# Six more pair sums ahead of the transposes, as accumulating transfers: a convolution stage on one Trainium2 core

## The reference

```python
# layer 0: attention over channels inside 8x8 windows, then a two-layer MLP, both residual
q, k, v = to_grid(conv1x1(x, Wq, bq)), to_grid(conv1x1(x, Wk, bk)), to_grid(conv1x1(x, Wv, bv))
attn = softmax(einsum('bgck,bgcl->bgkl', q, k) / sqrt(128))
x = x + from_grid(einsum('bgkl,bgcl->bgck', attn, v))
x = x + conv1x1(gelu(conv1x1(x, W1, b1)), W2, b2)
# layer 1: a 3x3 convolution whose kernel is made anew for each pixel from 16 sets
enh  = depthwise3x3(conv1x1(x, w_pw)) + b            # padded
h    = grouped_conv3x3(x)                            # 16 channels, split in h1, h2
att  = conv1x1(h1 * h2) * attgamma + conv1x1(x, w_211)          # 16 numbers per pixel
attk = einsum('bpn,nm->bpm', att, selfw)             # 64 groups x 2 x (2*9) weights per pixel
y    = einsum('bpgij,bpgj->bpgi', attk, patches3x3(enh)) + einsum('bpn,nc->bpc', att, selfb)
x    = y * ga1 + enh + x
```

## Time and profile before

| | before |
|---|---|
| median of three runs | 5735.58 us |
| the profiled execution: its own time | 5731.75 us |
| the profiled execution: its span | 5730.0 us |
| TensorE busy, matmuls | 5581.3 us (97%) |
| VectorE busy | 5083.3 us (89%) |
| GpSimd busy | 4185.7 us (73%) |
| ScalarE busy | 3463.1 us (60%) |
| share of the DMA engines used | 22% |

### The profile page before, as it was taken

How to read it: one execution, slowest core, us unless ns; L and a number is a source line. 1 busy time by engine, 2 the same in 40 slices (tenths; PEclk the granted TensorE clock), 3 DMA queues, 4 the chain that set the end, 5 groups by cost and what they waited for, 6 DMA issues and landing times.

```text
span 5730.0 us, 115887 instructions
## 1 busy us (share of the span) xinstructions
PE 5581.3 (97%) x39944; PEld 4131.5 (72%) x39944; DVE 5083.3 (89%) x5319; ACT 3463.1 (60%) x4284; POOL 4185.7 (73%) x1831
## 2 busy tenths in 40 slices
PE   8999999999998699999999999999999999999998
PEld 7888888888886366666666766666666666766666
DVE  7888888888887789999899998989999899998989
ACT  6888888888886455455554555555455554555553
POOL 4565555555654678888888888888888888888885
PEclk9999999999999799999999999999999999999999
DMA  2222222222221222222222222222222222222221
GB/s 89 73 73 73 73 73 77 77 73 73 73 73 62 52 72 67 69 64 65 73 67 70 62 65 71 67 71 66 68 64 65 73 67 70 62 65 71 67 71 45
DMA packets 155248, 394.20 MB, mean 69 GB/s; under 512 B 35136, under 2 KB 38400, under 8 KB 155136
## 3 DMA queue, kind: packets, MB, share of 16 engines
q1 hardware_dynamic: 154800, 392.87, 22.0%
q10 hardware_dynamic: 400, 0.69, 0.1%
HBM read 219.37 MB, written 136.31 MB: 62 GB/s over the span
## 4 chain that ended last, share of the span: by engine, by line
PE 54%; DMA 8%; DVE 3%; SPq 1%; issue 1%; ACT 1%; DVEq 0%; POOLq 0%; POOL 0%; ACTq 0%
PE ps_t L888 18%; PE ps_k L871 17%; DMA xin<-layer_out 8%; PE ps_m L854 8%; PE ps_p L840 5%; PE ps_t L905 2%; DVE products L1100 2%; PE ps_t L896 1%; PE ps_t L903 1%; PE ps_m L861 1%; ACT out_sb L991 1%; SPq L736 1%; DVE products L1062 0%; SPq L684 0%; SPq L711 0%
## 5 line engine op out<-in xcount | busy, mean ns | idle before, releaser
L805 POOL TENSOR_TENSOR enh<-enh,tap 128x1280 f32<-128x1280 f32 (+1 forms) x1024 | 2512.9, 2454 | 485.2 <-ACT tap L1009 431.7
L1100 DVE TENSOR_TENSOR products<-ps_k,enh 128x1024 f32<-128x1024 f32 x1792 | 2157.4, 1221 | 269.4 <-PE ps_k L871 248.5
L871 PE MATMUL ps_k<-att,basis 128*128 128x512 f32 x4608 | 1719.3, 459 | 22.1 <-DVE products L1100 10.9
L1009 ACT ACTIVATE tap<-e,dw 128x1280 f32<-128x1280 f32 (+1 forms) x1024 | 1260.6, 1251 | 0.0
L871 PEld LDWEIGHTS ps_k<-att,basis 128*128 128x128 f32 x4608 | 719.4, 190 | 701.2 <-DVE products L1100 451.1
L296 POOL TENSOR_TENSOR hidden_lo<-hidden,hidden_hi 128x1024 fp32r<-128x1024 f32 x256 | 693.1, 2726 | 717.2 <-DVE hidden_hi L501 717.2
L888 PE MATMUL ps_t<-ident_swap,products 128*128 128x128 f32 x6144 | 921.7, 273 | 0.0
L888 PE MATMUL ps_t<-ident,products 128*128 128x128 f32 x6144 | 919.7, 272 | 0.2 <-POOL products L811 0.2
L888 PEld LDWEIGHTS ps_t<-ident,products 128*128 128x128 f32 x6144 | 757.3, 140 | 175.7 <-POOL products L811 0.5
L811 POOL TENSOR_TENSOR products<-products 128x1024 f32<-128x1024 f32 x256 | 611.8, 2390 | 268.0 <-DVE products L1100 268.0
L888 PEld LDWEIGHTS ps_t<-ident_swap,products 128*128 128x128 f32 x6144 | 719.9, 141 | 0.0
(11 more groups left out here) (111 smaller groups left out, 7378.1 us busy)
## 6 DMA issues: line engine op xcount, KB each, us to landing
xin<-layer_out SPq DMA_DIRECT2D x64, 1280.0 KB, 7.2
xt<-in_x SPq DMA_DIRECT2D x128, 512.0 KB, 4.0
layer_out<-xo SPq DMA_DIRECT2D x128, 512.0 KB, 2.9
x_own<-layer_out SPq DMA_DIRECT2D x128, 512.0 KB, 4.0
out<-out_sb SPq DMA_DIRECT2D x256, 256.0 KB, 2.0
att<-att_hi SPq DMA_DIRECT2D x512, 32.0 KB, 1.9
att<-att_lo SPq DMA_DIRECT2D x512, 32.0 KB, 2.0
h_up<-h_sb SPq DMA_DIRECT2D x256, 16.0 KB
```

Source lines behind the costliest of these rows:

```text
L805: nc.gpsimd.tensor_tensor(own, own, tap_sb[add % TAP_BUFFERS][:, 0:hi - lo, :], ALU.add).then_inc(dw_done, 1)
L871: mm = nc.tensor.matmul(ps_k[KERNEL_BUFFER[q]][:, BANK * s:BANK * (s + 1)], basis[:, 2 * t + s, :], att[p][:, j, :], start=True, stop=True)
L1009: nc.scalar.activation(tap_sb[add % TAP_BUFFERS][:, 0:hi - lo, :], src, ACT.Copy, scale=dw[:, t:t + 1]).then_inc(tap_ready, 1)
L1100: nc.vector.tensor_tensor(out, kernels, enh[p][:, r:r + CHUNK_ROWS, dx:dx + W].unsqueeze(1).to_broadcast([C, 2, CHUNK_ROWS, W]), ALU.mult) ...
```

## The change

The pairs become sixteen: six on VectorE (two fewer), four on GpSimd (as many, other pairs), and six of a third kind. For a pair of the third kind GpSimd waits for the second product and issues a transfer inside SBUF whose data is added to the destination: 512 KB of product `q + 1` onto product `q`. TensorE's term waits for that transfer's semaphore. A band has 20 terms and 42 VectorE operations. The ring `products` gets a fifteenth place (4 KB more per partition). All order tables are replaced.

```diff
-PRODUCTS = 14
+PRODUCTS = 15
-VECTOR_MERGES = (0, 3, 10, 12, 18, 21, 27, 30)
-POOL_MERGES = (6, 15, 24, 33)
+VECTOR_MERGES = (0, 6, 11, 18, 24, 29)
+POOL_MERGES = (4, 13, 22, 31)
+DMA_MERGES = (2, 9, 15, 20, 27, 33)
+SUMMED_BEFORE = tuple(sorted(POOL_MERGES + DMA_MERGES))
-TERMS = [q for q in STORED if q - 1 not in POOL_MERGES]
+TERMS = [q for q in STORED if q - 1 not in SUMMED_BEFORE]
-TERM_SLOT = {1: 4, 2: 5, 4: 11, 5: 9, 6: 15, 8: 12, 9: 13, 11: 18, 13: 19, 14: 20, 15: 26, 17: 23, 19: 26, 20: 27, 22: 34, 23: 33, 24: 35, 26: 36, 28: 37, 29: 39, 31: 41, 32: 42, 33: 48, 35: 45}
+TERM_SLOT = {1: 2, 2: 17, 4: 12, 7: 11, 8: 10, 9: 16, 12: 16, 13: 23, 15: 27, 17: 21, 19: 25, 20: 34, 22: 33, 25: 30, 26: 36, 27: 45, 30: 38, 31: 47, 33: 49, 35: 46}
-BACK_SLOTS = [21, 30, 38, 54]
+BACK_SLOTS = [22, 31, 40, 54]
-POOL_MERGE_PLACES = (2.1, 4.5, 10.5, 13.45)
+POOL_MERGE_PLACES = (0, 4.0, 8.5, 11.0)
+DMA_MERGE_PLACES = (1.5, 1.7000000000000002, 5.2, 7.0, 10.2, 12.5)
-PW_SLOTS = [17, 22, 24, 29, 31]
+PW_SLOTS = [20, 22, 24, 29, 35]
...
+                def merge_by_dma(n, index):
+                    q = DMA_MERGES[index]
+                    pool.wait_ge(product_ready, SLOTS_IN_BAND * n + OP_COUNT["product", q + 1])
+                    pool.sem_inc(dma_merge_begun, 1)
+                    nc.gpsimd.dma_start(products[:, PLACE[q], :, :], products[:, PLACE[q + 1], :, :],
+                                        accum_op=ALU.add).then_inc(dma_merged[q], 16)
...
+                    elif q in DMA_MERGES:
+                        pe.wait_ge(dma_merged[q], 16 * n + 16)
...
+                    elif at - 1 in DMA_MERGES:
+                        at_least(dve, dma_merged[at - 1], 16 * before + 16)
```

More of the change, by code:

```diff
@@ L80 @@
 TERM_COUNT = {q: i + 1 for i, q in enumerate(sorted(VECTOR_TERMS, key=lambda q: (TERM_SLOT[q], q)))}
-BACK_SLOTS = [21, 30, 38, 54]
+BACK_SLOTS = [22, 31, 40, 54]
 POOL_PLACES = 2 * (TAPS - 1)
-POOL_MERGE_PLACES = (2.1, 4.5, 10.5, 13.45)
[L89 to L95, removed]
+POOL_MERGE_PLACES = (0, 4.0, 8.5, 11.0)
+DMA_MERGE_PLACES = (1.5, 1.7000000000000002, 5.2, 7.0, 10.2, 12.5)
+TAP_PLACES = ((0.5, 0.5, 1.5, 3.5, 8.5, 12.5, 13.5, 15.0, 15.0), (22.5, 23.0, 27.5, 29.5, 34.0, 38.0, 38.0, 42.4, 42.4))
+CLEAR_PLACES = (29, 59)
+H_PROD_SLOT = 24
+ATT_HIGH = 28
 ATT_LOW = 32
-CONV_SLOTS = [33, 33, 40, 40, 43, 43, 43, 43, 50, 50, 52, 52, 56, 56, 59, 59, 62, 62]
+CONV_SLOTS = [32, 32, 39, 39, 41, 41, 41, 41, 49, 49, 51, 51, 54, 54, 56, 56, 61, 61]
 COEFFICIENT_SLOT = 28
-PW_SLOTS = [17, 22, 24, 29, 31]
+PW_SLOTS = [20, 22, 24, 29, 35]
 def at_least(engine, semaphore, value):
@@ L657, in convolve @@
         pool_merged, pool_term_done = sem("pool_merged"), sem("pool_term_done")
+        dma_merge_begun = sem("dma_merge_begun")
+        dma_merged = {q: sem(f"dma_merged{q}") for q in DMA_MERGES}
         sum_done, sumT_ready, back_done, out_ready = sem("sum_done"), sem("sumT_ready"), sem("back_done"), sem("out_ready")
@@ L811, in merge @@
                     nc.gpsimd.tensor_tensor(lead, lead, products[:, PLACE[q + 1], :, :], ALU.add).then_inc(pool_merged, 1)
+                def merge_by_dma(n, index):
[4 more added lines that the diff above has]
+                                        accum_op=ALU.add).then_inc(dma_merged[q], 16)
                 ORDER = ([(t - 1, add_tap, 1, (0, t)) for t in range(1, TAPS)] +
                          [(TAPS - 1 + t - 1, add_tap, 1, (1, t)) for t in range(1, TAPS)] +
-                         [(place, merge, 2, (i,)) for i, place in enumerate(POOL_MERGE_PLACES)])
+                         [(place, merge, 2, (i,)) for i, place in enumerate(POOL_MERGE_PLACES)] +
+                         [(place, merge_by_dma, 2, (i,)) for i, place in enumerate(DMA_MERGE_PLACES)])
                 def step(items, p):
@@ L820, in step @@
                         if items[k] is not None:
-                            if action is merge:
+                            if action in (merge, merge_by_dma):
                                 action(items[k], *args)
```

## The result

The changed kernel takes 5698.28 us (median of four runs, 5697.71 to 5701.17) against 5738.16 us before on the same chip: a ratio of 0.9928, 95% interval 0.9916 to 0.9940. It is 40 us faster. I had forecast 160 us, so the direction was right and the size was not. The profiled execution took 5698.64 us by its own time.

What follows compares the result with a forecast made beforehand. TensorE was taken as the bound at 59.22 us a band; 59.22 - 3.5 + 0.3 + 1.2 - 0.5 = 56.7, about 160 us off, forecast 5578 us. Range of 8 in 10: 5485 to 5810.

Steps and rivals of the forecast that it cites:

- What bounds the kernel: TensorE, busy 58.4 us of a 59.22 us band, is the bound, with VectorE 5 us behind.
- Four terms at 0.87 us: 24 terms on TensorE become 20, which takes 3.5 us a band off it.
- The closer race with VectorE: VectorE stays 4.4 us below TensorE instead of 5.6: 0.3 us a band charged, bounds 0 and 1.2.
- GpSimd's price, d = 1.0: Each of six new transfer issues holds GpSimd 1.0 us, giving 54.5 us of work; it sets the pace from 1.4.
- rival 2: GpSimd's issue price well above 1.4 us makes GpSimd the bound; at 2.4 the kernel takes 5970; chance 0.21.
- The landing: TensorE waits at term 9 for the transfer onto product 10's pair: 0.1 + 1.0 + 5.9 - 5.8 = 1.2 us a band.
- L: Time for an adding transfer's data to land, taken as 5.9 us, bounds 3.2 and 9.5.
- Small edits: TensorE's wait for `xin` gains 0.5 us a band; the ring adds no new VectorE wait, bounds 0 and 0.2.
- The sum: All terms together give 56.7 us a band, 160 us off the kernel, 5578 us.
- Rival 1: The transfer lands early, under 4.7 us, so no wait at term 9: 55.4 us a band, 5491; chance 0.24.
- rival 3: Contested landing of 8.2 us, so term 9 waits 3.5 us a band: no change, 5735; chance 0.15.
- Rival 4: VectorE already paces TensorE, so removed transposes buy nothing: about 5700, sign VectorE above 95%; chance 0.07.

Runs made afterwards that it cites:

- the best version: The changed kernel with `h_prod` at slot 27 instead of 24 and the term of pair 9 in slot 18 instead of 16: 5522.80 us.
- both edits: The changed kernel with `h_prod` moved from slot 24 to 27 and the term of pair 9 from slot 16 to 18: 5522.80 us, ratio 0.9623.
- the kernel with ten sums: The kernel with `h_prod` at slot 27 and term 9 in slot 18, its six transfers replaced by six sums on GpSimd: 5957.35 us.
- the experiment: The changed kernel with one number altered, `h_prod` at slot 27 instead of 24: 5581.40 us, ratio 0.9727.

## Why the prediction was wrong, step by step

- **What bounds the kernel: right.** TensorE was the bound. With the two new waits gone a band takes 55.93 us, where the floor was put at 55.7.
- **Four terms at 0.87 us: right.** Six terms more cost 5.12 us, 0.85 each.
- **The closer race with VectorE: too low.** The floor of 55.7 us less the 0.6 us of `xin`, which is gained in full, is 55.1; the best version takes 55.93. That leaves 0.8 us where 0.3 were charged, inside the bounds of 0 and 1.2. It is a remainder: no run measures this term by itself.
- **GpSimd's price, d = 1.0: right within its bounds**, 0.85 measured. 48.5 + 6 x 0.85 are the 53.6 us that GpSimd has to do, not 54.5. What I held against rival 2, that the same kind of work holds SyncE for 0.7 us at most, overlooked a line of the earlier trace rows: one issue there holds SyncE for 2.40 us, which is rival 2's price. That d came out near the cheap rows was luck in this respect. The sums done by transfer are what keeps GpSimd under the bound: in the kernel with ten sums a band takes 62.79 us, where rival 2's sum gave 62.9 for 2.4 us each.
- **The landing: right in kind, size 1.2 us against 0.9, partly by luck.** From `h_prod` at 27 alone to both edits a band falls by 0.94 us. I reckoned 0.1 + 1.0 + 5.9 = 7.0 us from the product to the landing. By the trace GpSimd starts the issue 0.6 us after product 10, and the data land 6.7 us after that start, the issue included: 7.3 us. So L was put too low, the issue was counted twice, and the two errors nearly cancel. The Trainium skill (DMA: Bandwidth & Descriptors, "Anatomy of one DMA — SWDGE (gpsimd) path") gave 3.2 us for a copy, and 2.9 were measured. From the rule of the Trainium skill (Collectives: The Full Stack, "The bandwidth ceiling: the fold count and why AG ≠ RS ≠ AR") that an addition reads two sources, I had estimated 4.4 us for an addition; the median of all six is 4.7 and the least 4.5, and the queue's share on the DMA engines doubled, 28.7% against 13.8%. That fits. For the one transfer that counts, at 5.9 to 7.7 us, the estimate was too low, and the first rival, whose missing wait it stood for, did not come.
- **Small edits: this step failed.** I went through the edits that remove or add a wait for `xin` and the ring, and did not price the three single slots, `H_PROD_SLOT` among them, though the text ahead of the prediction says that they are shifted. They stand in the sum at nothing, without a reason. The grouped convolution's last piece moved from slot 18 of the step to 19 and `h_prod` from 27 to 24: nine slots became five. VectorE waits 2.3 us a band for it, and by the experiment it costs 58.78 - 56.87 = 1.91 us a band, 117 us. How well it was covered could be read in the trace of before: ScalarE's `h_sb` at 3034.20, four issues that end at 3037.65, and `h_prod` at 3042.53, 8.3 us after `h_sb` began. In the changed kernel VectorE is there 4.5 us after `h_sb` begins (3020.8 less 3016.33), less than the copy, the four issues and even a landing of 2 us take together.

```profile
3034.20 0.69 ACT L966 ACTIVATE h_sb<-ps_m,bias_h 128x512 f32<-128x512 f32 x1
```

```profile
3042.53 0.74 DVE L1120 SCALAR_TENSOR_TENSOR h_prod<-ps_m,bias_h,h_up 128x512 f32<-128x512 f32 x1
```

- **And the traffic was charged to the wrong reader.** I asked what 512 KB more on the DMA engines do to `xin` and to the transfer itself, and not what they do to four transfers of 16 KB on SyncE's queue, which are on a short path. This delay is two thirds of the wait: 1.6 of 2.3 us. It comes from one adding transfer that GpSimd issues just ahead of them, not from the loads that I had in mind as the rivals for the DMA engines.
- **The sum.** Without that one wait it is right: 5578 forecast, 5581.4 measured with `h_prod` at 27. That it fits to 4 us is luck in part: 0.5 us too little for the closer race stands against 0.3 too much for the landing and 0.1 too little for `xin`. In the changed kernel 0.44 us a band are left of the 2.5.
- **Rivals.** Rival 1 did not come; its 55.4 us is near what both edits reach. Of rival 3 the mechanism is there, a contested landing, but at 6.7 us and not 8.2, and its wait of 3.5 us is not. Rival 4's time, about 5700, is the measured one, and its mechanism is not: it wanted VectorE above 95%, and VectorE is busy for 50.8 of 58.78 us; what holds TensorE up is one wait of VectorE's, and with that gone the four terms pay. Its number came by coincidence. The measured time lies in the range of 8 in 10, 5485 to 5810, and outside the likeliest case's own, 5530 to 5640; the gain was a quarter of the forecast.

Open: why the clock falls after some of the gaps of 2.2 us and not after others. TensorE is busy for 0.3 us a band more than in the best version (55.82 against 55.50); the rest of the 2.85 us between them is idle time. Also open is the cost of five slots by itself in the old order, since no run moved ScalarE's two taps.

## What to carry to other kernels

When a table that sets the order is replaced as a whole, every entry in it is an edit. For each I would write down who produces what it waits for, over how many hops, and compare the distance in slots with the path's duration in the old trace, the short side branches first. Additional traffic is to be charged to every transfer in flight beside it, above all to small ones behind which a busy engine waits. A median over all issues of a line can hide the one that counts: here 4.7 us over six transfers, and 6.7 for the one with a term close behind. And a wait that is taken away alone may show nothing: the term's two slots gave nothing before `h_prod` was moved, and 59 us after.

## What the runs showed of the hardware

- An adding transfer of 512 KB inside SBUF, issued from GpSimd, holds it for 0.85 us and lands in 4.7 us in the median, 4.5 at least, counted from the issue's start; a copy takes 0.57 and 2.9 us; an eighth of the data, added, 0.85 and 2.4 us. The issue's price depends on the addition and not on the bytes. Issued 1.1 to 1.8 us behind another and with loads going out beside it, the adding transfer took 5.9 to 7.7 us.
- A transfer of 16 KB that lands in 1.96 us takes 4.58 and 3.13 us in the two bands read of the changed kernel, 2.8 to 4.6 us over 42 bands, with one adding transfer of 512 KB in flight beside it.
- An addition of GpSimd behind such an issue looks longer and is not slower: it starts 0.25 us before the issue's end and takes 2.48 us, where the same addition elsewhere takes 2.21. From the issue's end to its own it is 2.23 us.

```profile
3037.52 0.86 POOL L835 DMA_DIRECT2D products<-products  x1 [1.01 <-DVE products L1130]
3038.13 2.48 POOL L823 TENSOR_TENSOR enh<-enh,tap 128x1024 f32<-128x1024 f32 x1
...
3045.24 2.21 POOL L823 TENSOR_TENSOR enh<-enh,tap 128x1024 f32<-128x1024 f32 x1
```

- In one band a gap of 2.17 us in TensorE's work was followed by 4 us at a granted clock of 0.57.
